# Loading and splitting Wx in the middle of a factor stream instead of near its end

## The reference

```
c = layernorm(cond) * gamma + beta
h = gelu(c @ W1 + bias1)
w = h @ W2 + bias2                       # W2: 512 x 16384, 32 MB
a1, b1, a2, b2 = split(w, 4)             # each (16, 512, 8)
mid = gelu(x @ base_down + (x @ a2) @ b2^T)
x1  = x + x + mid @ base_up^T + (mid @ b1) @ a1^T
xW  = x1 @ Wx + b
for t in range(512):
    h_t = tanh(xW[:, t] + h_{t-1} @ Wh)
out = x1 + h
```

## Time and profile before

| | |
|---|---|
| median of 3 runs | 1230.5 us (1229.95 to 1232.67) |
| profiled execution, its own time | 1231.63 us |
| span of the profiled execution | 1229.9 us |
| TensorE busy / weight load busy | 1184.4 us / 955.7 us |
| VectorE / ScalarE / GpSimd busy | 867.1 / 679.0 / 253.1 us |
| mean granted TensorE clock | 0.975 of full speed |
| W2 loads on the queue of SyncE | 1024 KB each, 8.9 us median from issue to landing |

### The profile page before, as it was taken

One profiled execution on the slowest core, in us unless ns is written; L12 is line 12 of the kernel. 1 busy time (PEld: TensorE's weight loads), 2 busy tenths in 40 slices (PEclk: granted clock), 3 DMA queues, 4 the chain that ended last, 5 costly groups with the idle time before them and its releaser, 6 DMA issues.

```text
span 1229.9 us, 50560 instructions
## 1 busy us (share of the span) xinstructions
PE 1184.4 (96%) x20920; PEld 955.7 (78%) x20920; DVE 867.1 (71%) x3637; ACT 679.0 (55%) x2649; POOL 253.1 (21%) x523
## 2 busy tenths in 40 slices
PE   7877999999999999999999999999999999999996
PEld 6344888888888888888888888888888888888764
DVE  5424577777777777777777777777777777777564
ACT  2122565656566656666565666566665656565442
POOL 0000122222222222222222222222222222222111
PEclk6698999999999999999999999999999999999998
DMA  8998211312121211213122212212131222011012
GB/s 246 408 409 269 41 20 19 54 20 43 31 37 27 38 28 33 41 20 54 20 39 35 37 23 37 34 30 43 20 54 20 37 36 34 7 20 20 6 33 36
DMA packets 284085, 75.72 MB, mean 62 GB/s; under 512 B 273072, under 2 KB 273088, under 8 KB 283856
## 3 DMA queue, kind: packets, MB, share of 16 engines
q1 hardware_dynamic: 277488, 71.89, 24.9%
q10 hardware_dynamic: 6368, 0.60, 0.4%
HBM read 55.68 MB, written 16.78 MB: 59 GB/s over the span
## 4 chain that ended last, share of the span: by engine, by line
PE 89%; DMA 5%; ACT 2%; DVE 2%; SPq 1%; issue 1%; ACTq 0%; DVEq 0%; POOLq 0%; POOL 0%
PE bulk L953 45%; PE rec L969 33%; PE bulk L956 5%; DMA work<-in_L_cond_W_dram 5%; PE bulk L942 2%; ACT hf L616 1%; PE bulk L931 1%; SPq L446 1%; DVE z L834 1%; PE bulk L891 1%; ACT rec L544 1%; DMA hf<-in_L_cond_b_dram 0%; DVE work L801 0%; PE bulk L1067 0%; DVE wx_s L679 0%
## 5 line engine op out<-in xcount | busy, mean ns | idle before, releaser
L969 PEld LDWEIGHTS rec<-hs,wh_s 128*128 128x128 f16 x16352 | 442.7, 96 | 135.7 <-DVE hs L842 134.1
L616 ACT ACTIVATE hf<-z,scl 128x32 f32<-128x32 f32 x1024 | 274.0, 315 | 410.7 <-DVE z L834 405.5
L969 PE MATMUL rec<-hs,wh_s 128*128 128x32 f16 x16352 | 493.4, 177 | 6.9 <-ACT rec L544 6.7
L501 POOL TENSOR_TENSOR work<-work,hf 128x64 f32<-128x64 f32 x512 | 251.7, 492 | 966.2 <-DVE hs L842 966.2
L834 DVE TENSOR_REDUCE z<-rec 128x32 f32<-128x96 f32 x1022 | 233.8, 258 | 136.3 <-PE rec L969 121.4
L839 DVE TENSOR_SCALAR hs<-hf 128x32 f16<-128x32 f32 x1024 | 182.2, 178 | 99.6 <-ACT hf L616 99.6
L953 PE MATMUL bulk<-mid_s,up_s 128*128 128x512 f32 x768 | 223.0, 410 | 0.0
L842 DVE SCALAR_TENSOR_TENSOR hs<-hf,hs 128x32 f16<-128x32 f32 x1024 | 196.8, 192 | 35.3
L953 PE MATMUL bulk<-act_x,down_s 128*128 128x512 f32 x768 | 220.0, 410 | 0.0
L953 PE MATMUL bulk<-act_s,wx_s 128*128 128x512 f32 x768 | 210.1, 407 | 0.0
L544 ACT ACTIVATE rec<-work 128x32 f32<-128x32 f32 x1022 | 183.3, 209 | 0.0
(11 more groups left out here) (106 smaller groups left out, 674.1 us busy)
## 6 DMA issues: line engine op xcount, KB each, us to landing
work<-in_L_cond_W_dram SPq DMA_DIRECT2D x33, 1024.0 KB, 8.9
work<-in_x_dram SPq DMA_DIRECT2D x256, 64.0 KB, 3.5
out_dram<-work SPq DMA_DIRECT2D x248, 64.0 KB, 2.3
work<-in_L_cond_base_up_dram SPq DMA_DIRECT2D x1, 1024.0 KB, 7.9
work<-in_L_cond_base_down_dram SPq DMA_DIRECT2D x1, 1024.0 KB, 10.4
work<-in_L_cond_Wh_dram SPq DMA_DIRECT2D x1, 1024.0 KB, 12.9
work<-in_L_cond_Wx_dram SPq DMA_DIRECT2D x1, 1024.0 KB, 9.1
out_dram<-work ACTq DMA_DIRECT2D x8, 64.0 KB, 3.4
```

Source lines behind the costliest of these rows:

```text
L501: nc.gpsimd.tensor_tensor(xs, xs, hf[:, t % 4], ALU.add).then_inc(sum_done, 1)
L616: nc.scalar.activation(hf[:, t % 4, half], z[:, half], ACT.Tanh, scale=inv).then_inc(tanh_done, 1)
L969: last = nc.tensor.matmul(R[fo][:, m, 0:PARTS, :], wh_s[:, q, k, n * P:(n + 1) * P], hs[:, k, :, :], start=(m == k == q == 0), stop=(k == ...
```

## The change

Two tables of numbers are altered. Wx becomes entry 14 of the ring instead of 30, so that it follows W2's half tile 11; ScalarE's copy moves to slot 13 and VectorE's subtraction to slot 14. The entry that has to wait for Wx's buffer is now 18, half tile 15, instead of 34, half tile 31. Half tiles 12 to 27 are loaded one entry later than before. The products of TensorE and their order stay as they are.

```diff
-WX_HI_AT, WX_LO_AT = 28, 29
+WX_HI_AT, WX_LO_AT = 13, 14
...
-        WX_ENTRY = HALVES + 2 - 4
+        WX_ENTRY = 14
```

## The result

| | before | after |
|---|---|---|
| median | 1230.5 us (1229.95 to 1232.67, 5 runs) | 1236.65 us (1236.19 to 1238.38, 5 runs) |
| ratio after / before | | 1.0046, 95% interval 1.0034 to 1.0058 |
| profiled execution, own time / span | 1231.63 / 1229.9 us | 1236.19 / 1234.5 us |

Slower by 0.46% (5.7 us, 4.2 to 7.1). I had forecast 1231.8 in a range up to 1234.8, 65% on no difference.

The account below looks back on a forecast made before the run. W2 landings (in one place Wx) pace the start, with DMA nearly full; TensorE's recurrence passes shifts on. Half tile 31 +4.1, clock at the end -2.8, sum +1.3 on 1230.5 gives 1231.8 us; range 1230.0 to 1234.8.

Parts of the forecast that it names:

- which wait, where, and that it ends up as a later half tile 31: At entry 18, SyncE waits for Wx's split with 16 W2 loads behind; half tile 31 at 118.6 against 114.50, +4.1 us.
- So the old place costs 2.3 us of stream: At entry 34 in the kernel before: half tile 31 starts at 114.50 instead of 112.19 at the cadence.
- Its clock part at the end: From half tile 31 to the last xw product, full instead of half TensorE clock: -2.9 us, counted as -2.8.
- entry 18 is issued at 72.1: At the new gap: Wx's split ends at 72.1, entry 18 lands 5.09 us later at 77.2, a 6.0 us gap.
- I expect 0.50 in roughly 75 to 87: TensorE around the new gap: idles 5.8 us, so half tiles take 1.94 us instead of 1.07, hidden under the cadence.
- Half tile 31. It is 16 entries behind entry 18: 77.2 + 16 x 2.57: Stream behind the new gap: cadence of 2.57 us an entry puts half tile 31 at 118.3; 118.6 was taken.
- The 0.2 us that it had for the drain of the last load: End of the stream: a drain may cost some tenths more, so half tile 31 was taken at 118.6, not 118.4.
- Cost: nothing, and that slack is the cover: Behind the new gap: a late TensorE releases buffers in time, with 3.8 us of slack (8.9 against 5.09).
- The longer restart: Rival at entry 18: it lands after 6.68 us instead of 5.09, +1.6, hence 1233.4 us; chance 0.14.
- The low clock at the end: Rival from half tile 31 on: clock stays low, all of +4.1 us stays, 1234.6 us; chance 0.17.
- A low clock under slot 19: Rival: low clock outlasts slot 19, TensorE 8.7 us late at half tile 20, second gap 4.9, 1236.7 us; chance 0.06.
- Faster: Rival at entry 18: loads in flight cover the gap if issued before 68.7; with no gap 1225.4 us; chance 0.05.

Follow-up runs that it names:

- late_own_buffer: Kernel before (Wx late, split in slots 28 and 29) with Wx loaded into a buffer outside the ring; 1227.33 us, ratio 0.9964.
- mid_own_buffer: Changed kernel with Wx loaded into a buffer outside the ring, split still in slots 13 and 14; 1229.72 us, ratio to before 0.9989.
- mid12_hold_x: Changed kernel with Wx's split in slots 12 and 13 and second-chunk x loads held until entry 34 has landed; 1229.72 us, ratio to before 0.9981.
- theory L: Tested on the changed kernel, split in slots 12 and 13, by adding extra TensorE products ahead of half tiles 12 and 13; 1230.22 against 1230.25 us without them.
- the run with x held: Changed kernel with the second chunk's x loads issued only after entry 34 has landed; 1236.88 us, ratio to before 1.0050.
- mid_split12: Changed kernel with ScalarE's copy of Wx in slot 12 and VectorE's subtraction in slot 13, one slot earlier; 1230.25 us, ratio to before 0.9992.

## Why the prediction was wrong, point by point

**Right: which wait, where, and that it ends up as a later half tile 31.** SyncE holds entry 18 for the split; 16 loads of W2 stand behind it. The run with the wait put back by hand shows it alone.

**Right: what the old place cost the stream.** "So the old place costs 2.3 us of stream": 2.26 in S. Its clock part at the end, forecast 2.9 and counted as 2.8, was 3.2 in the chain of the profiled execution (from half tile 31's start to the last xw product 141.15 - 122.33 = 18.82 against 136.50 - 114.50 = 22.00) and 2.2 us in the measured time. In that chain the 24 products took 5.46 us, where I had scaled them to 5.98. Together 5.1 forecast; 4.4 measured (3.0 to 6.0), by the late kernel without a pause.

**Mis-sized: "entry 18 is issued at 72.1", and 77.2 for its landing.** Measured 73.52 and 79.01. Of the 1.4 us, 1.1 is the clock, and 0.2 is that the stream began later in this execution. I had written "I expect 0.50 in roughly 75 to 87", behind the new pause, and had taken the 1.00 and 1.47 us to slot 13's transposition and factor copy from a stretch at full clock. But the load of Wx itself makes TensorE wait (2.54 and 1.09 us ahead of half tiles 12 and 13), the clock falls between 64 and 65, and half tile 13 with its transposition takes 2.6 instead of 1.4. I had the idle time at hand, half tile 12 moved one cadence later with the same work in front of it, and looked for a low clock only where the pause was. From its issue to half tile 15's start it took 5.49 us, where entry 34 of the kernel before took 5.13 (5.09 to the landing).

**Wrong step: "Half tile 31. It is 16 entries behind entry 18: 77.2 + 16 x 2.57".** The 16 entries took 122.33 - 79.01 = 43.32 us, 2.71 each, though the DMA moved 410 GB/s from 79 to 99 and no second pause came. The 16 completion events that each load leaves in the trace say why. This table is worked out from them: the spread between the first and the last of the 16, in us.

```
entry          9    10    17    18    22    23    31    33    34
before        0.5   1.9   1.9   1.9   1.9   1.9   2.0   1.9   0.6
after         0.5   1.8   1.8   0.9   1.0   2.1   2.4   2.3   3.1
```

A load is there only when its slowest part is. In the full stream of the kernel before, the slowest part runs late by a constant 1.9 us, which does not show in a cadence. A pause lets it catch up (0.9 at entry 18, 0.6 at entry 34 of the kernel before), and behind the pause the lag builds up again. The first parts of entries 18 and 34 landed at 78.11 and 119.20, 41.1 us apart, which is 16 cadences of 2.57; the other 2.2 us of the 43.32 are the growth of the spread from 0.9 to 3.1. I had joined a landing on an empty queue to a cadence from a drifted stream. So the sum had the catching up in it (the 5.09 us of entry 34 was such a landing) and left out the relapse. The 0.2 us that it had for the drain of the last load stands on no row; the spread grew by 0.8 us from entry 33 to 34 in the kernel after and by nothing in late_own_buffer.

The Trainium skill, "DMA: Bandwidth & Descriptors", section on queues, rings and completion order, says that one copy is split over up to 16 rings, each worked off by its own engine; the table agrees, and shows 16 events a load. Why the lag grows in steps was not tested. Instruction loads (a page's queue q8), each one packet of 16 KB that takes 1.1 us, lie ahead of the steps at entries 10, 23, 31 and 34 of the kernel after. In the kernel before, where the spread stays at 1.9, those at 64.7, 77.5 and 95.3 are each followed by one more part that lands over 1 us behind the first: two such parts from entry 10 on, then three, four and five of the 16. That speaks for the instruction loads, but no run takes them away: argued, not shown.

**Wrong: "Cost: nothing, and that slack is the cover"** for the middle place. Without any pause the middle place gives ratios of 0.9981 to 0.9992, the late place 0.9964 to 0.9978. Three pairs give the place's price, each with its interval: own buffer 3.1 us (1.2 to 5.0), split one slot earlier 2.7 (1.1 to 4.3), the latter with x held 1.2 (-0.5 to 2.9). In the first pair more than the place differs: in late_own_buffer SyncE waits for the split of Wx before it issues the loads of x, so that they go out 2.8 us before the last load of the stream has landed, in mid_own_buffer 8.5 us before. So the place costs something between one and three us; how much is open.

In S the pairs give 2.1, 0.9 and 0.8, and the landings say where it went. In the own-buffer pair 0.3 of the 2.1 is in the first parts (77.23 us from half tile 2 to half tile 31 against 76.89) and 1.8 in the lag of the last load (its spread was 3.8 us against 1.7). In the split pair the first parts were 0.2 us faster in the middle place, and the lag took 1.1. So in these executions most of it is the lag. Why the lag is larger in the middle kernels is open. Their spreads at entries 23 to 31 are mostly 2.4 to 3.3, but 1.9 in mid12_hold_x; in the late kernels they are 1.7 to 2.2. Late release of ring buffers may play a part: in mid_own_buffer half tiles 17 to 20 landed 6.4 to 8.2 us after their issue instead of about 9, and the DMA moved 305 GB/s in 80 to 82. With 8.9 us to landing against 5.1 on an empty queue I counted 3.8 us of slack, but the parts that run early have 1.9 less of it. Whether the low clock is behind it is open too (theory L above). No run separates these.

**The account.** In the profiled executions half tile 31 came 7.65 us later by S (88.18 - 80.53) where I had 4.1. Of the 3.55 us missed, 1.2 are the later issue of entry 18, 0.4 its landing, and 1.9 the 16 entries behind it. The stretch from half tile 31 to the last xw product gave back 3.2 instead of 2.8. That makes +4.5 where I had +1.3; the median ratio says 5.7 (4.2 to 7.1).

The same loss can be cut by kernels. From the late place without a pause: before +4.4 us (its pause and clock), after 3.1 (place) and 7.0 (from 0.9989 to 1.0046) = +10.1; the difference is the measured 5.7, by construction, since it comes from the same ratios. My sum had +6.4 for the new pause against 7.0 to 7.8 measured, -5.1 for the old one against -4.4, and 0 for the place against 3.1 by this pair and 1.2 to 2.7 by the others. The place and the lag are not two losses to be added: most of the place's price in S is lag.

**The rivals.** None of them was the case in the profiled execution of the changed kernel. The longer restart was partly so (5.49, not 6.68). The low clock at the end came in six of the other profiled executions, behind the last transposition and for 1.6 us, and not from half tile 31 on for 2.8. A low clock under slot 19, with a short second gap of the DMA behind it, came in the run with x held (92 to 96, and 98 to 100). That rival's 1.4 us for slot 17's 12 products is 1.1 by its own row (three times 0.38), which makes its 1236.7 into 1236.4. "Faster" needed entry 18 issued before 68.7: in mid_split12 it was, at about 65.5, and the result was still no more than equal, since the place's own cost was missing in that rival too.

## What to carry to other kernels

A transfer that waits for more than the queue ahead of it has a price at its place in the queue: ask what is issued behind it, and whether the instruction that releases it stands behind a later landing on its own engine; if so, move the release ahead, which here was two numbers (27, 28) and worth 3.7 us, where the change of place lost 5.7. Do not extend a landing measured after a pause by the cadence of a full stream: the slowest of the parallel parts sets both, and in these traces a pause took its lag away (1.9 to 0.9 and 0.6 us) and it came back (3.1). And when a transfer is moved into a stream, look for what idles while it passes, not only for the wait that it brings.

## What the runs showed of the hardware that I had not expected

The slowest of the 16 parts of each 1 MB load lagged the first by 1.5 to 2.2 us in the full stream of the late kernels, from entry 10 on and nearly constant within each execution; up to entry 9 it was 0.3 to 1.6 us. In the kernel before the number of parts over 1 us late grew from two to five on the way, by one behind each instruction load. The clock behind half tile 31 fell in some executions and not in others of kernels that differ little there (20.4 against 18.8 us for that stretch). Executions of one kernel also differ by up to 5 us (1228.73 to 1234.15 over 12); the slowest of these, the only one profiled, had its DMA engines partly idle at a full clock (307 and 274 GB/s above). Why is open.
